# Order of TensorE's work in an attention step: the second maxima's scores ahead of the product with v

## The reference

```python
qkv = jnp.einsum('bld,ed->ble', xn, w_qkv)            # 16 heads of 16 channels
q, k = rope(q), rope(k)
scores = jnp.einsum('blhd,bmhd->bhlm', q, k) / 4      # 2048 x 2048 for each of 64 (sequence, head)
attn = jax.nn.softmax(scores, axis=-1)
out = jnp.einsum('bhlm,bmhd->blhd', attn, v)
y = x + out_projection(out) + ffn(xn)                 # ffn: silu(gate) * up, hidden 768, integer weights
```

## Time and profile before

| | us |
|---|---|
| median of 3 runs | 2934.07 |
| lowest and highest | 2931.21, 2934.49 |
| profiled execution | 2935.97 |
| its span in the trace | 2934.2 |
| PE busy | 2854.9 |
| DVE busy | 2667.8 |
| ACT busy | 2480.9 |
| granted clock of PE, mean | 0.99 |

### The profile page before, as it was taken

One profiled execution on the slowest core, in us unless ns is written; L12 is line 12 of the kernel. 1 busy time (PEld: TensorE's weight loads), 2 busy tenths in 40 slices (PEclk: granted clock), 3 DMA queues, 4 the chain that ended last, 5 costly groups with the idle time before them and its releaser, 6 DMA issues.

```text
span 2934.2 us, 67972 instructions
## 1 busy us (share of the span) xinstructions
PE 2854.9 (97%) x27582; PEld 1052.0 (36%) x27582; DVE 2667.8 (91%) x2946; ACT 2480.9 (85%) x4639; POOL 636.2 (22%) x1214
## 2 busy tenths in 40 slices
PE   6999999999999999999999999999999999999997
PEld 4666664333333333333333333333333333333334
DVE  7667666999999999999999999999999999999952
ACT  4544555999999999999999999999999999999972
POOL 4666673011111111111111111111111111111110
PEclk9999997999999999999999999999999999999999
DMA  3233331111111111111111111111111111111125
GB/s 116 86 96 116 100 95 55 25 31 31 31 31 31 31 31 31 31 31 31 31 31 32 31 31 31 32 31 31 31 31 31 31 31 31 31 31 31 31 66 177
DMA packets 128700, 137.18 MB, mean 47 GB/s; under 512 B 43264, under 2 KB 111488, under 8 KB 128384
## 3 DMA queue, kind: packets, MB, share of 16 engines
q1 hardware_dynamic: 128384, 132.79, 16.7%
HBM read 88.15 MB, written 34.08 MB: 42 GB/s over the span
## 4 chain that ended last, share of the span: by engine, by line
PE 86%; ACT 5%; DVE 4%; issue 2%; DMA 1%; POOL 0%; SPq 0%; POOLq 0%; DVEq 0%; ACTq 0%
PE psum L764 37%; PE psum L729 21%; PE psum L800 17%; PE psum L635 5%; PE psum L606 4%; ACT probs L966 3%; ACT acc_sb L936 1%; DVE row_max L1390 1%; PE psum L650 1%; ACT hT L860 1%; DVE stats L1139 1%; PE psum L710 0%; DVE xnT L1163 0%; DVE h L1305 0%; DMA out_y<-y_in 0%
## 5 line engine op out<-in xcount | busy, mean ns | idle before, releaser
L1390 DVE TENSOR_REDUCE row_max<-psum 128x1 f32<-128x1024 f32 x2018 | 2297.2, 1217 | 23.8 <-PE psum L729 23.8
L966 ACT ACTIVATE probs<-psum 128x512 f32<-128x512 f32 x4096 | 2179.2, 595 | 159.2 <-PE psum L800 52.9
L764 PE MATMUL psum<-probs,v_op 128*32 128x256 f32 x15872 | 1297.6, 399 | 0.0
L800 PE MATMUL psum<-q_op,k_op 51*128 51x512 f16 x4096 | 854.4, 381 | 20.7 <-ACT probs L966 15.6
L729 PE MATMUL psum<-k_op,q_op 48*128 48x512 f16 x4066 | 808.0, 389 | 5.2 <-DVE row_max L1390 2.7
L729 PEld LDWEIGHTS psum<-k_op,q_op 48*128 48x128 f16 x4066 | 196.7, 93 | 853.1 <-DVE row_max L1390 543.5
L764 PEld LDWEIGHTS psum<-probs,v_op 128*32 128x32 f32 x15872 | 312.5, 108 | 525.2 <-issue 493.4
L800 PEld LDWEIGHTS psum<-q_op,k_op 51*128 51x128 f16 x4096 | 365.2, 94 | 252.3 <-ACT probs L966 70.9
L1118 POOL TENSOR_TENSOR acc_sb<-acc_sb,inv_rows 128x512 f32<-128x512 f32 x64 | 81.7, 1276 | 1682.1 <-DMA inv_rows<-inv_dram 1682.1
L635 PE MATMUL psum<-xnT,wf 128*128 128x512 f16 x768 | 179.0, 379 | 0.5 <-DVE v_space L1295 0.5
L867 ACT ACTIVATE parts<-qk_rot 128x512 f16<-128x512 f32 x64 | 40.2, 628 | 149.0 <-POOL qk_rot L1036 149.0
(11 more groups left out here) (121 smaller groups left out, 1200.6 us busy)
## 6 DMA issues: line engine op xcount, KB each, us to landing
qk_dram<-staged SPq DMA_DIRECT2D x64, 256.0 KB, 4.9
q_op<-qk_dram SPq DMA_DIRECT2D x128, 128.0 KB
k_op<-qk_dram SPq DMA_DIRECT2D x128, 128.0 KB
x_ln<-in_x SPq DMA_DIRECT2D x16, 512.0 KB, 4.4
x_res<-in_x SPq DMA_DIRECT2D x16, 512.0 KB, 5.3
y_dram<-y_blk SPq DMA_DIRECT2D x16, 512.0 KB, 3.4
k_op<-qk_dram SPq DMA_DIRECT2D x128, 64.0 KB
q_op<-qk_dram SPq DMA_DIRECT2D x128, 64.0 KB
```

The lines of the kernel that those rows point to most:

```text
L764: mm = pe.matmul(bank(7)[32 * j:32 * j + 32, n0:n1], v_op[:, h % 2, t, :], probs[:, g3 % PROBS, j * BANK + n0:j * BANK + n1], start=(t == ...
L800: pe.matmul(bank(b), k_op[r:e, h % SLOTS, t * P:(t + 1) * P], q_op[r:e, h % SLOTS, j * BANK:(j + 1) * BANK], start=True, stop=True).then_i ...
L966: nc.scalar.activation(probs[:, g2 % PROBS, j * BANK:(j + 1) * BANK], bank(b), ACT.Exp, scale=to_score).then_inc(s2_used, 1)
L1390: nc.vector.tensor_reduce(row_max[:, hl % 2, t, half:half + 1], psum[:, 2 * half * BANK:(2 * half + 2) * BANK], AX.X, ALU.max).then_inc(s1 ...
```

## The change

In steps with a product with v (g2 >= 2) and with maxima (c < 1024), the two matmuls of the second half of the maxima are issued ahead of part 0 of the product with v in place of behind it. Steps 0 to 20 and the steps from 1024 on keep their order. What each instruction computes and waits for stays the same.

```diff
             for j in range(4):
                 if j == 2:
+
+                    early = g2 >= PV_LAG
+                    if early and c < N1:
+                        max_half(c, 1)
                     weigh_v(0)
-                    if c < N1:
+                    if not early and c < N1:
                         max_half(c, 1)
                     h = head_of(c, STAB_AT)
                     if h is not None:
```

## The result

The changed kernel takes 2997.7 us (median of 4, 2996.43 to 2998.41) against 2934.28 for the kernel before on the same occasion (4 runs): ratio 1.0219, 95% interval 1.0207 to 1.0231. That is 63 us slower, where 61 were forecast (2995).

The account below looks back on a forecast made before the run. DVE was taken to set the pace except at two places a head. Sixteen steps of 2.305 plus 0.39, 0.49 and 0.05 gave 37.81 us a head, 61 us more in all: 2995 us, range 2948 to 3022.

Parts of the forecast that it names:

- The loop: Ordinary steps: reduces, release, second maxima, PE work, next first maxima, landing; 4.61 us for two steps, 2.305 each against 2.26.
- The alternation: Ordinary steps on DVE: the loop's slower copy sets the pace, so first reduces start 2.27 and 2.34 us apart in turn.
- The transpose: Step transposing the stabilisers, score 3 held by ACT's exponential: next maxima 0.39 us late per head, bounds 0.16 and 0.51.
- The save: Saving a head's sum after the long last product: next step's second maxima 0.49 us late, bounds 0.3 and 0.7.
- The reciprocal: Reciprocal on DVE, partly hidden by idle time: 0.05 us a head, between 0 and 0.24.
- The sum: Whole head: 37.81 us against 36.84, 0.97 more, times 62.7 heads 61 us; 2995 us, given 60%.
- 1: Rival: loop stays under DVE's pace, only irregular places cost; 0.41 us a head, 26 us, 2960 us; chance 21%.
- 2: Rival: faster, as second maxima ahead of the 1.00 us product remove DVE's idle; up to 30 us, 2910; chance 9%.
- 3: Rival: weight load bare behind the moved wait on PE, +0.10 us in the loop, 50 us more, 3045; chance 5%.
- 4: Rival: PE's waits lower its granted clock; one head in ten at the lower level adds over 100 us; chance 1%.
- 5: Rival: nothing changes because the DVE floor hides it, 2934 us; chance 4%.

Follow-up runs that it names:

- e1: Changed kernel with the second maxima moved ahead of the product in even steps only: 3004.48 us, 1.0249 to the kernel before.
- e2: Changed kernel with the next step's first maxima also issued ahead of their half of the product: 2945.21 us, 1.0042 to the kernel before.
- e3: Changed kernel with the second maxima directly behind the first, ahead of scores 0 and 1 too: 3213.28 us, 1.0957 to the kernel before.
- e5: Changed kernel with DVE's second reduce at half its columns from step 21 on, exponent scaled by a quarter: 2943.76 us, 1.0039 to the kernel before.
- e8: Changed kernel with DVE's stabiliser wait moved one half-step earlier, in front of the last head's last reduce: 2998.3 us, 1.0226 to the kernel before.
- e7: Kernel before with the second maxima moved ahead only in the step with a head's long last product: 2956.07 us, 1.0082.
- e6: Kernel before, old order, with DVE's second reduce at half its columns and the same scaled exponent: 2931.79 us, 0.9997.
- e9: Kernel before with the stabilisers' transpose moved behind the product, ACT's copy and SP's DMA wait moving with it: 2989.44 us, 1.0193.

## Why the prediction was right, point by point

- **The loop.** Forecast 2.305 a step, measured 2.3125 (4.625 for two). The one unseen spacing, maxima to product, was taken at 0.31 and is 0.32, and so is scores to product. Its form is shown by e1 (half the moves, same loss), e2 (distance 1.11, no loss), e3 (longer path, longer steps) and e5 (shorter reduce, 51 of 63 us gone). Over 16 steps the term was 0.12 too small.
- **The alternation.** Forecast 2.27 and 2.34, measured 2.27 and 2.35. PE's waits were put at 0.13 and 0.06; from the timeline they are 0.13 (scores to second maxima 0.35) and 0.03 (0.25). The second is shorter because a fed DVE starts its second reduce 1.13 after the first and not 1.14, so the release comes 2.40 after the first reduce in place of 2.42, and because the longer step is 2.35.
- **The transpose.** Forecast 0.39, measured 2.66 - 2.35 = 0.30 (from unrounded medians). The step's own account was right: the next maxima come 2.50 after the first scores (1528.93 to 1531.43), as forecast, and e8 has 2.72 - 2.35 = 0.37; most of the difference is the next point.
- **A head's border.** Not forecast: 2.42 in place of 2.35, 0.07. e8 shows that it is DVE's second wait. The transpose gives the 0.07 back, so the two together are 0.37 where 0.39 stood.
- **The save.** Forecast 0.49, measured 2.80 - 2.35 = 0.44. Score 1 of the next step comes 2.84 after the first scores in place of 2.89:

```profile
1536.29 0.38 PE L804 MATMUL psum<-q_op,k_op 51*128 51x512 f16 x2
...
1539.13 0.39 PE L804 MATMUL psum<-q_op,k_op 51*128 51x512 f16 x1 [0.45 <-ACT probs L970]
```

- **The reciprocal.** Forecast 0.05, measured nothing: the steps around it take 2.42 + 2.20 = 4.62, as any two. In the kernel before it costs 0.10, 4.62 against 4.52.
- **The sum.** 37.00 + 0.07 + 0.30 + 0.44 = 37.81, which is the number forecast. The hit is closer than the terms: the loop was 0.12 short, the others together 0.12 long, and that they cancel is luck. With the few heads that have an odd wait more the mean is 37.87. The loss is a little larger than forecast, too: 0.97 a head was 37.81 less a mean of 36.84, while mean to mean it is 1.03, and median to median (37.82 and 36.77) 1.05. I would trust the method to some 0.15 a head, 10 us.
- **Rivals.** 1 (the loop free) is out by the 4.625; 2 (faster) by e7, where the stall at the long product goes and a longer one comes; 3 (a bare weight load) by the 0.32; 4 by the clock; 5 by the time.
- **What bounds the kernel before.** Here the prediction was only half right. It had PE faster than DVE by 0.02 in a half-step and "never waits for a free bank in the steady part", so that DVE set the pace but for two places a head. Its half-step of 1.11 is one of two kinds: the other takes 1.14, because score 3 waits for its bank (1514.23 to 1514.57), and PE's whole step is 2.247 (e6), not 2.21 to 2.22, against DVE's 2.262. So the lead grows by 0.015 a step, not 0.04, and e6 shows that a head takes 36.77 with a DVE that is busy 80% of the time (1598.3 of the 2000 us from 700 to 2700). The forecast survived this because the loop, at 2.3125 a step, is longer than either.

## What to carry to other kernels

Where two engines alternate over a pair of buffers, follow one buffer round: end of use, release, everything that stands in the queue up to the next refill of the other buffer, landing, use. An order that leaves each engine's sum of work alone can still lengthen that ring, and here it cost because the ring took 4.62 us for two steps where DVE needed 4.52, and spreading the refills evenly (e2) was what kept it short. And an edit at a stall moves it unless the slack behind it is followed too: e7, e8 and e9 each cured the place that they aimed at, and none was faster than the kernel that it started from.

## What the runs showed of the hardware that was not expected

- A second semaphore wait in front of a reduce cost nothing where DVE was fed (2.26 at a head's border in the kernel before, as in any ordinary step) and 0.07 us where it was starved (2.42 against 2.36 at a head's border, e8).
- A 0.24 us reciprocal between two reduces cost a starved DVE nothing in two steps (4.62 with and without it); DVE in the kernel before paid 0.10 for it.
- PE issued the eight product matmuls 0.32 us behind a pair of maxima, and the same behind a pair of scores, also right after a wait for DVE; the weight load of the waiting matmuls added nothing that can be seen (load and matmul both at 1529.35).
